# Feed-forward turn with the route at its head, and the second stage's input sums taken in attention

## The reference

```
x = x + 0.5 * ffn(layernorm(x))
x = x + attention(layernorm(x))      # causal, over 4096 rows of each of the 2 batches
x = x + 0.5 * ffn(layernorm(x))      # the same weights again

ffn(n):
    xm     = mix0 * n[s-1] + mix1 * n[s] + mix2 * n[s+1]        # neighbours along the sequence
    scores = tanh(xm @ Wo1 + bo1) @ Wo2 + bo2                   # 9 scores for each row
    path   = argmax(scores)                                     # one of 9
    h      = xm @ W1[p] + b1[p]          # 64 wide, for all 9 paths
    y      = h[path] @ W2[path] + b2[path]
    return layernorm(n + y, gamma, beta)

attention(n): q, k, v projections; weights = softmax(|q k| / 16) below the diagonal; out @ Wo + bo
```

## Time and profile before

| what | value |
|---|---|
| median of 3 runs | 1528.1 us (1524.33 to 1539.24) |
| the profiled execution | 1531.81 us, its span 1530.0 us |
| first feed-forward stage | 0 to about 335 us |
| attention, two batches | about 335 to 1212 us |
| second feed-forward stage | about 1212 to 1530 us |
| mean granted TensorE clock | 0.967 of full |

### The profile page before, as it was taken

How to read it: one execution, slowest core, us unless ns; L and a number is a source line. 1 busy time by engine, 2 the same in 40 slices (tenths; PEclk the granted TensorE clock), 3 DMA queues, 4 the chain that set the end, 5 groups by cost and what they waited for, 6 DMA issues and landing times.

```text
span 1530.0 us, 25980 instructions
## 1 busy us (share of the span) xinstructions
PE 1359.1 (89%) x7700; PEld 781.4 (51%) x7700; DVE 1215.7 (79%) x2349; ACT 936.8 (61%) x1745; POOL 306.9 (20%) x359
## 2 busy tenths in 40 slices
PE   4889988858999999999968999999998779989985
PEld 2556666544554454545344455454444346656653
DVE  6989999766677677677866767777678769999985
ACT  5656665326567666566855666766666666666642
POOL 2244452332001000000041101000000214444311
PEclk9989999979999999999989999999999879999997
DMA  5143333320000100102110011000103112333221
GB/s 155 43 118 88 90 101 113 90 69 1 28 29 15 41 14 15 32 11 74 37 43 1 28 42 42 0 28 0 42 0 110 56 32 61 103 97 106 61 74 57
DMA packets 86994, 82.26 MB, mean 54 GB/s; under 512 B 8540, under 2 KB 86885, under 8 KB 86885
## 3 DMA queue, kind: packets, MB, share of 16 engines
q1 hardware_dynamic: 86884, 80.91, 17.8%
HBM read 55.43 MB, written 25.46 MB: 53 GB/s over the span
## 4 chain that ended last, share of the span: by engine, by line
PE 62%; DVE 11%; DMA 10%; issue 7%; ACT 6%; SPq 2%; POOL 1%; DVEq 0%; ACTq 0%; POOLq 0%
PE PS L1324 55%; DMA R<-oh_scratch 7%; PE PS L1501 3%; DMA oh_scratch<-oh_t 2%; DVE R L753 2%; PE PS L1389 2%; PE PS L1332 1%; DVE R L770 1%; DVE R L937 1%; SPq L414 1%; SPq L412 1%; ACT oh_t L1113 1%; ACT R L1211 1%; ACT R L1215 1%; ACT R L1174 1%
## 5 line engine op out<-in xcount | busy, mean ns | idle before, releaser
L1324 PE MATMUL PS<-R 128*128 128x512 f16 (+3 forms) x3456 | 713.6, 361 | 27.4 <-DVE R L937 17.3
L1324 PEld LDWEIGHTS PS<-R 128*128 128x128 f16 (+1 forms) x3456 | 326.0, 98 | 392.3 <-DVE R L937 32.0
L1324 PE MATMUL PS<-w_hi,R 128*128 128x256 f16 x1280 | 239.1, 280 | 63.3 <-DVE R L753 63.1
L937 DVE TENSOR_TENSOR R<-R 128x512 f16<-128x512 f32 (+3 forms) x288 | 188.6, 655 | 111.5 <-ACT R L1215 110.3
L1202 ACT ACTIVATE R<-PS 128x512 f32 (+5 forms) x288 | 160.2, 558 | 162.7 <-PE PS L1324 162.2
L1324 PE MATMUL PS<-R,w_hi 128*128 128x512 f16 x640 | 198.0, 392 | 1.6 <-DVE R L747 1.5
L1211 ACT ACTIVATE R<-R 128x512 f32 (+4 forms) x288 | 169.5, 589 | 48.3 <-DVE R L931 46.8
L931 DVE TENSOR_TENSOR R<-R,max_row 128x512 f32 (+4 forms) x288 | 187.1, 650 | 7.7 <-ACT max_row L1248 7.7
L1215 ACT ACTIVATE R<-R 128x512 f16<-128x512 f32 (+3 forms) x288 | 171.1, 594 | 28.6 <-ACT R L1211 2.6
L925 DVE TENSOR_TENSOR run_max<-run_max,R 128x512 f32<-128x512 f32 (+3 forms) x272 | 173.9, 639 | 10.0 <-DVE run_max L925 1.7
L1324 PEld LDWEIGHTS PS<-w_hi,R 128*128 128x128 f16 x1280 | 128.4, 100 | 104.5 <-DVE R L753 77.1
(11 more groups left out here) (109 smaller groups left out, 1555.3 us busy)
## 6 DMA issues: line engine op xcount, KB each, us to landing
R<-x_scratch SPq DMA_DIRECT2D x48, 512.0 KB, 4.5
x_scratch<-R SPq DMA_DIRECT2D x32, 512.0 KB, 3.2
R<-oh_scratch SPq DMA_DIRECT2D x32, 320.0 KB
R<-in_L_attn_x SPq DMA_DIRECT2D x16, 512.0 KB, 5.4
R<-oh_scratch SPq DMA_DIRECT2D x32, 256.0 KB
out<-R SPq DMA_DIRECT2D x16, 512.0 KB, 3.2
R<-in_L_ffn_W SPq DMA_DIRECT2D x2, 288.0 KB
R<-in_L_ffn_W SPq DMA_DIRECT2D x1, 512.0 KB
```

The costliest lines, as they stand in the source:

```text
L937: v.tensor_tensor(p_lo[:, i * TT + lo:(i + 1) * TT], pf[:, (i % 2) * TT + lo:(i % 2 + 1) * TT], p_hi[:, i * TT + lo:(i + 1) * TT], ALU.sub ...
L1324: ins = t_.matmul(dst, w, xx, start=start and n == 0, stop=stop and n == last, skip_group_check=skip)
```

## The change

In the feed-forward turn:

- **PE.** `route(t+2)` opens the turn, `choice(t+2)` follows `path(t, 0)`. The router's chunk is made a turn earlier and late in it: `hidden(t+3, 0)` stands behind `path(t, 3)` and `transposed(t+5)`, ahead of `path(t, 4)`. `h_order` follows.
- **DVE.** Behind `result(t-1)` come the five steps of `route(t+2)`; in ph 0 the four `bn_stats` of tile t+6 stand between them. Then mixing, the moments, the second half of the mixing, `masked` 0 and 1, `mixed_low`, `masked_low` 0, `masked` 2, 3 and 4, `masked_low` 1, and the last three steps as before.
- **ACT.** `scores`, `middle`, `squares`, `one_hot`, `normalised`, `x_high`, the three `masked_high`, `transposed`.
- **POOL.** `residual(t)` opens the turn and waits for the second product of tile t-1 (`o_psum`) instead of the fourth masked chunk; `norm_scale` and `result_scale(t-1)` follow.
- **SP.** The order is as it was; `mask_in` is two semaphores, one for each mask buffer.

In ph 1 no sums are taken from the rows. Attention takes them: `output_sums` is one `bn_stats` for each part of each output tile, behind the next part, and for all 16 tiles; they lie in `x2_st`. The store of the tile and the waits of ACT, POOL and PE for the end of attention go by the new `x2_sums`. The moments of tiles 5 to 15 read `x2_st`; the first five tiles still have their own sums.

```diff
+FIRST = ROUTE + 1
@@ the order of the hidden chunks' banks
-                h_order += [(use(ph, t + ROUTE), 0)] if on(t + ROUTE) else []
                 h_order += [(use(ph, t + HIDDEN), c) for c in range(1, HC)] if on(t + HIDDEN) else []
+                h_order += [(use(ph, t + FIRST), 0)] if on(t + FIRST) else []
@@ SP, spread(t)
-                        sp.wait_ge(mask_in, 16 * MASK_LOADS * (g - 1))
+                        sp.wait_ge(mask_in[g % 2], 16 * MASK_LOADS * (g // 2))
@@ SP, attention, store(j)
-                    sp.wait_ge(x2_done, SUB * s + SUB)
+                    sp.wait_ge(x2_sums, SUB * s + SUB)
@@ POOL, residual(t) and turn(t)
-                    pool.wait_ge(hm_done, HC * k + 4)
+                    if t >= 1:
+                        pool.wait_ge(o_psum, k)
...
-                    if on(t - 1):
-                        result_scale(t - 1)
-                    if on(t + HIDDEN):
-                        residual(t + HIDDEN)
+                    if on(t):
+                        residual(t)
...
+                    if on(t - 1):
+                        result_scale(t - 1)
@@ DVE, ffn
+                def input_sum(t, u):
                     n = counted(ph, t)
-                    dve.wait_ge(x_in[t % NT], 16 * loads(ph, t))
-                    if n >= 2:
-                        dve.wait_ge(n_shift, n - 1)
-                    row_sums(X, t % NT * SUB * D, rows_set(ph, t), n_stat)
+                    if u == 0:
+                        dve.wait_ge(x_in[t % NT], 16 * loads(ph, t))
+                        if n >= 2:
+                            dve.wait_ge(n_shift, n - 1)
+                    ins = v.bn_stats(st[:, rows_set(ph, t), u, :], cols(x_rows(t), u * D, D))
+                    if u == SUB - 1:
+                        ins.then_inc(n_stat, 1)
                 def input_moments(t):
...
+                    dve.wait_ge(x2_sums, SUB * NTT)
+                    dve.wait_ge(n_shift, n - 1)
+                    for u in range(SUB):
+                        ins = v.bn_aggr(mv[:, rows_set(ph, t), u, :], sums_at(t, u))
+                    ins.then_inc(n_var, 1)
@@ DVE, turn(t), behind result(t - 1)
+                    for i in range(SUB + 1):
+                        if choice:
+                            route(t + ROUTE, i)
+                        if ph == 0 and rows and i < SUB:
+                            input_sum(t + STATS, i)
+                    if mix:
+                        mixed_before(t + MIX, 0)
+                        mixed_before(t + MIX, 1)
+                    if rows:
+                        input_moments(t + STATS)
...
+                        mixed_behind(t + MIX, 0)
+                        mixed_behind(t + MIX, 1)
                     if here:
                         masked(t + HIDDEN, 0)
                         masked(t + HIDDEN, 1)
                     if mix:
+                        mixed_low(t + MIX)
...
                         masked_low(t + HIDDEN, 0)
                         masked(t + HIDDEN, 2)
                         masked(t + HIDDEN, 3)
                         masked(t + HIDDEN, 4)
                         masked_low(t + HIDDEN, 1)
@@ DVE, attention, output(s, u)
+                    if u >= 1:
+                        output_sums(s, u - 1, rows)
+                    if u == SUB - 1:
+                        output_sums(s, u, rows)
+                def output_sums(s, u, rows):
+                    dve.wait_ge(x2_done, SUB * s + u + 1)
+                    v.bn_stats(sums_at(s, u), cols(rows, u * D, D)).then_inc(x2_sums, 1)
@@ PE, turn(t)
+                    if choose:
+                        route(t + ROUTE)
                     if second:
                         hidden(t + HIDDEN, 1)
                     if here:
                         path(t, 0)
+                    if choose:
+                        choice(t + ROUTE)
...
                         path(t, 3)
+                    if on(t + ROWS):
+                        transposed(t + ROWS)
...
+                    if on(t + FIRST):
+                        hidden(t + FIRST, 0)
+                    if here:
                         path(t, 4)
```

More of the change, by code:

```diff
@@ L217, in macaron @@
         xr_in, x2_done, x2_stored = sem("xr_in"), sem("x2_done"), sem("x2_stored")
+        x2_sums = sem("x2_sums")
         block = ctx.enter_context(nc.Block())
@@ L228, in attention_over @@
         def attention_over(eng):
-            wait_apart(eng, x2_done, SUB * NTT)
+            wait_apart(eng, x2_sums, SUB * NTT)
         BLOCKS = SUB * NT * (NT + 1) // 2
@@ L701, in row_moments, with sums_at @@
                 ins.then_inc(var_done, 1)
+            def sums_at(tile, u):
+                return cols(x2_st, within(dve, (tile * SUB + u) * 6, (NTT * SUB - 1) * 6), 6)
             def first_stats(n, tiles):
@@ L799, in masked @@
                     if c == 0:
-                        dve.wait_ge(mask_in, 16 * MASK_LOADS * (g + 1))
+                        dve.wait_ge(mask_in[g % 2], 16 * MASK_LOADS * (g // 2 + 1))
                         dve.wait_ge(hb_done, g + 1)
@@ L824, in turn @@
                     if mix:
[L825 to L828, removed]
+                        mixed_low(t + MIX)
                     if here:
                         masked_low(t + HIDDEN, 0)
-                    if choice:
-                        route(t + ROUTE, 1)
-                    if here:
                         masked(t + HIDDEN, 2)
[L835 to L845, removed]
-                        masked(t + HIDDEN, 3)
-                    if rows:
-                        input_sums(t + STATS)
-                    elif first_of(ph, t):
-                        first_stats(0, first_of(ph, t))
-                    if mix:
-                        mixed_low(t + MIX)
-                    if here:
+                        masked(t + HIDDEN, 3)
                         masked(t + HIDDEN, 4)
-                    if rows:
-                        input_moments(t + STATS)
-                    if here:
                         masked_low(t + HIDDEN, 1)
@@ L1065, in normalised @@
                         act.wait_ge(n_shift, counted(ph, t) + 1)
+                    if ph == 1 and not early(ph, t):
+                        act.wait_ge(x_in[t % NT], 16 * loads(ph, t))
                     if t >= NT:
@@ L1137, in turn @@
                         act.wait_ge(w1_ready, 1)
+                    if choice:
+                        scores(t + ROUTE)
                     if mix:
                         middle(t + MIX)
-                    if choice:
-                        scores(t + ROUTE)
-                    if here:
-                        masked_high(t + HIDDEN, 0)
                     if last:
                         squares(t - 1)
+                    if choice:
+                        one_hot(t + ROUTE)
                     if on(t + ROWS):
@@ L1149, in turn @@
                         x_high(t + MIX)
-                    if choice:
-                        one_hot(t + ROUTE)
                     if here:
+                        masked_high(t + HIDDEN, 0)
                         masked_high(t + HIDDEN, 1)
+                        masked_high(t + HIDDEN, 2)
                     if on(t + ROWS):
                         transposed(t + ROWS)
-                    if here:
-                        masked_high(t + HIDDEN, 2)
                 for t in turns():
@@ L1414, in turn @@
                 def turn(t):
-                    here, second, first = on(t), on(t + HIDDEN), on(t + ROUTE)
-                    if ph == 0 and t == -ROUTE:
-                        pe.wait_ge(w1_ready, 1)
+                    here, second, choose = on(t), on(t + HIDDEN), on(t + ROUTE)
                     if ph == 0 and t == 0:
                         pe.wait_ge(w2_ready, 1)
-                    if first:
-                        hidden(t + ROUTE, 0)
+                    if choose:
+                        route(t + ROUTE)
                     if second:
@@ L1425, in turn @@
                         path(t, 0)
-                    if first:
-                        route(t + ROUTE)
+                    if choose:
+                        choice(t + ROUTE)
                     if second:
@@ L1435, in turn @@
                         path(t, 2)
-                    if first:
-                        choice(t + ROUTE)
-                    if on(t + ROWS):
-                        transposed(t + ROWS)
                     if second:
```

20 lines of the change are left out of this document (14 added, 6 removed).

## The result

| | median of its runs, us | ratio to before, 95% interval |
|---|---|---|
| before | 1526.2 (1524.1 to 1539.2) | |
| the change | 1570.9 (1568.3 to 1573.6) | 1.0275 [1.0213, 1.0336] |

The change makes the kernel 2.8% slower. The forecast was 1540, and the median stands 0.9 us above the upper end of the range, 1570: 44.7 us more than before, where 12 were forecast. The profiled execution of the changed kernel is 1569.6 us with a span of 1567.8 us, 37.8 us longer than the span of before; its mean granted clock is 0.960 (0.967 before).

The account below looks back on a forecast made before the run. DVE was taken to bound the feed-forward turns, held by POOL's L553. Ph 0 +28, ph 1 -21 and attention +5 gave +12, so 1540 us on the median of 1528.1; forecast 1532 to 1550 (chance 0.50), range 1510 to 1570.

Parts of the forecast that it names:

- What bounds the kernel now: Feed-forward turns: DVE works 17.09 of 17.16 us; POOL's L553 holds L747, costing 1.16 us in nearly all turns.
- Where R lies in turns 2 to 9: Ph 0: rows land 5.1 us into the turn, DVE stands 3.9; last route step (R) at 6.8, turn at least 20.3.
- The clock in those turns: Ph 0, turns 2 to 9: PE idles 4.4 us, clock falls in most; mean turn 22.2 us, +36 (+21 to +40).
- rival 1: Ph 0, turns 2 to 9: the clock stays up, turns 20.3 us, sum -3, 1525 us; chance 0.17.
- Ph 1's steady turn: Ph 1, turns 1 to 12: L553 holds the third route step, turn 16.44 us, together -8.5 us.
- The tail: Ph 1's last turns: L553 no longer lies between chunk 3 and the rest, -6.5 us.
- Rival 2: POOL's L553 gets in ahead of L770, held 2.4 us; turns alternate 18.8 and 15.9; 1554, up to 1570; chance 0.20.
- The starts: Ph 1: startup -4 us, turns -1 and 0 together -2; ph 0: turns -1, 0 and 1 together -4.5.
- A: Cause named for the experiments: in ph 0 the sums wait for the load, and the clock follows.
- B: Cause named for the experiments: POOL's addition of beta holds DVE in new places.
- Attention: 64 bn_stats, 21 us, added to DVE in attention, mostly hidden in its waits for PE: +5 us (bounds 0 and +21).
- C: Cause named for the experiments: the sums taken in attention.

Follow-up runs that it names:

- e6: The kernel before without GpSimd's beta addition, beta missing from the output: 1512.9 us, ratio 0.9905.
- e1: The change with ph 0's row sums moved back behind masked chunk 3, moments behind chunk 4, and POOL's last scale ahead of the input scales: 1549.7 us, 1.0136.
- e8: The change with POOL's beta addition beside the masked chunks, behind the next tile's masked_low 0 and ahead of norm_scale: 1550.8 us, 1.015.
- e3: The change with ph 0's sums late (DVE as in e1) and the beta addition beside the masked chunks (POOL as in e8): 1518.1 us, 0.9928.
- e7: The change with 16 unused extra matmuls on PE ahead of choice in turns 2 to 9 of ph 0: 1567.5 us, 1.0272.
- e5: The kernel before, with attention taking ph 1's input sums and ph 1's turns taking none: 1534.8 us, 1.006.
- e10: The change without the beta addition, only its semaphore increment kept, beta missing from the output: 1551.5 us, 1.0146.
- e2: The change with POOL's beta addition last in its turn, behind norm_scale and result_scale, waiting for the next tile's masked_low 0: 1574.8 us, 1.0314.

## Why the prediction was right in kind and where it was wrong

**What bounds the kernel now.** The held L747 was read rightly as too long, but "1.16 us in nearly all turns" was not what it cost: e6 shows 0.25 us a turn. DVE busy for 17.09 of 17.16 us meant only that DVE's chain came last, not that PE's was far behind. This did not enter the sum, since the new turn was counted from its own slots. PE's idle time in such a turn was 1.80 us and not 1.9.

**Where R lies in turns 2 to 9.** The load wait came as worked out: D+5.1 forecast, D+5.23 found in turn 6, standing 3.9 forecast and 3.91 found (3.69 to 5.20 over the eight turns). It is what the change loses most by, and e1 shows it (30.2 us) with e8 against e3 as a second pair (1550.8 and 1518.1 us, the eight turns 171.8 and 135.4).

**The clock in those turns.** It fell in every turn, as forecast, and rival 1 is out. The size was too large: most turns were low for about 3 us and not over the whole stretch that rows 11 and 12 suggested, so the turn was near 20.9 and not 22.5. The eight turns gave +29.7, inside the bounds of +21 and +40, and e7 puts 7.5 of it on the clock where the term had 15. That term's overcharge hid part of what the starts and tails lacked. And its premise, with the earlier trace rows, doesn't hold each time: the same stand of 2.85 us in e5 left the clock at 1.00. With e7 the fall in the change is tied to the stand, but what decides for a single stand stays open. The page "TensorE: Matmul & The Clock Gate" of the Trainium skill (HAM oscillation) had been quoted for a fall in every tile, and the trace bears this out for a stand that comes in every turn: 0.91 in the windows, 1.00 in e7's.

**Ph 1's steady turn** was 16.29 to 16.30 against the forecast 16.44. Its parts were right in kind: L767 free, the third route step held to 0.76, a wait of 0.47 for ACT's high part (0.58 forecast). Turns 2 to 12 gave 9.4 us against 7.8 forecast.

**The tail is the step that failed.** "The tail, where L553 no longer lies between chunk 3 and the rest: -6.5" came out at +3.7, and the last six turns of ph 0 at +5.0 instead of -3, together 18 us where the whole sum, with errors both ways, was 26 short. The prediction worked the -6.5 out from no row. Rival 2 had the mechanism, POOL let in ahead of a DVE instruction with two SBUF inputs, but I priced it for the steady turns, where it never happened, and not for the last ones, where PE has no transposes and no router's chunk left to make, the products are complete during `result_scaled`, and L558 is let in between two of the four. That reason is argued from the program's order; it doesn't say why turn 11 of ph 0, where the router's chunk is still made, is hit and turn 12 isn't. Five groups of +2.1 us were seen, and e8 and e10 show the whole cost in these stretches: 9.5 us in ph 0 and 7.0 in ph 1 (39.1 instead of 46.1). The five groups make 10.4 of these 16.5 us. Most of the rest lies in turn 14 of either stage, which e8 has at a higher granted clock: 21.91 us at 0.85 against 18.15 at 0.97 in ph 0, 19.26 at 0.77 against 14.49 at 1.00 in ph 1. With that gone the tail of ph 1 is 3.3 shorter than before, half of what I had claimed.

**The starts** were the second failure: ph 1's startup with turn 1 gave -0.7 and not about -7, and ph 0's +1.8 and not -4.5. The way to turn 1 of ph 0 was 69.2 us before (68.6 and 69.4 in the other two runs with the old order) and 72.9 in the change (73.0 to 76.5 in the eight runs on it, whether A or B is undone or not), so this is a loss of the new order itself, of 3.4 us or more, of which turn 1 gives 1.8 back. In the change DVE's wait for the first scores grew there from 3.13 to 5.61 us, and L767 waits 1.12 and 1.30 us for ACT. Why, and why filling the wait for the first mask gave nothing in ph 1, stays open: no run was made for this. I take it that a start is paced by the loads, the sums and the first route.

**Attention** was +7.4 against +5 (bounds 0 and +21), much as in e5 alone (+7.1), so C is shown.

The sum: 30.2 from A and about 20 from B, some 7 from C and a few from the start of ph 0, against the gain of the new turn, which is what e3 keeps. Had the tails been counted as they came, the forecast would have been 1540 + 18 = 1558. That it came near the range's end at all owes something to the clock's term, 6 us too high in turns 2 to 9.

## What to carry to other kernels

A step that is moved to the head of a turn takes its inputs' arrival with it: work out when the newest input lands, counted from the turn's start, before the step is put in front of work on which everything depends. Here a GpSimd pass over SBUF was free beside VectorE instructions with one input in PSUM (1550.8 us in e8, 1551.5 without the pass) and cost some 20 us beside those with two SBUF inputs; place it by a semaphore of the work that it shall lie beside, and put it ahead of GpSimd's small operations, not behind them. A pipelined loop's first and last turns have another mix of work than its steady ones, so a race priced there must be priced again for them. Two delays that overlap hide each other: undoing one alone showed 21 and 20 us here, undoing both 53.

## What was not expected of the hardware

- **When POOL is let in.** In the steady turn L558 asks at 1396.16, DVE goes from one instruction with two SBUF inputs to the next at 1396.52, and POOL isn't let in until 1397.6 (its end, 1399.95, less 2.37 of its own), when DVE comes to L773 with its PSUM input; in the tail it asks at 1523.62 and is let in ahead of the last of the four L782, which is held. The Trainium skill ("SBUF — State Buffer", section on who interferes with whom) speaks of issue order, which fits the second and not the first. What decides between the two stays open; no run told it apart.
- **How short the fall of the clock can be.** With a stand of 4.1 us in each turn, PE came back to 2.4 GHz after about 3 us, and lost 0.5 to 0.9 us of the turn by it in five turns, 1.5 to 1.9 in three; the single stand of 2.86 us of before had cost 4.5 (21.70 less 17.16), and the same stand in e5 nothing.
- **Small operations of POOL are held too.** L534 on 128 x 4 numbers takes from 0.23 us (e2) to 2.17 (e1), as L530 with 2.15 did before. In e2 the chain of five small operations ahead of the addition took it from 1409.50 to 1415.63, onto L831; the length of such a chain follows from where DVE's instructions lie more than from its own work.
